# Two fused layers on one core: weights first, head stacks built in place, expert choice without the wide reciprocal, projections over four banks

## The chip, the cores and the metric

One core of one Trainium2 chip. The metric is the device time of one execution of the program, in microseconds; the median of several runs is compared.

## What is computed

The input x is 8 batches of 512 tokens with 128 features. Each batch goes through two pre-norm layers, `x = x + L(layernorm(x))`, in f32.

```
attention layer (A), 16 heads, DH = 8:
  Q = split(x); K = split(x @ Wk + bk); V = split(x @ Wv + bv)
  o = softmax(Q K^T + causal) V
  y = x + gelu(o) @ Wf + bf
mixture layer (F), 8 heads of 64, 8 experts:
  q, k = x @ w_q, x @ w_k
  gates = sigmoid(x @ w_gate); sel = argmax over the experts, per head and token
  values = chosen gate * (x @ value_expert[sel])
  out = softmax(q * 0.125 k^T, causal) values
  y = sum over heads of chosen gate * (out @ output_expert[sel])
```

## The kernel before

The program is written out by hand, engine by engine, with counting semaphores: each engine runs its own list, and a semaphore counts on over all batches. Nothing reorders the work; the tables at the top (`BANK`, `VALUES_AT`, `MAX_AT`, `HOTS_AT`, `OUTPUTS`) say after which unit another layer's or batch's piece is put in. A batch runs: attention A, `turn` (gelu and projection back), `experts` with `project_f` on TensorE (the mixture layer's gates, q and k, and the expert values), attention F, in which the next batch's layer A is prepared; the output experts' products of the mixture layer are spread over attention F and the next batch's attention A. The last batch's products stand at the end.

Precision is made from parts. Scores of A: q and k are split into three bf16 parts, written to DRAM (`parts_to_dram`) and read back as stacks of 72 rows (`restack_q`, `restack_k`), with three rows more for the negated maxima and their ones (`maxima_rows`, L350). Scores of F: q and k are each split into a high half, made by ScalarE (L926), and a low half, made by VectorE (L1276), in `pt`; `restack_f` (L339) sends both from there to four stacks: `s1q` (q high, q low), `s1k` (k high twice), `s2q` (q high) and `s2k` (k low), heads in pairs, 12 DMAs a pair, always to rows 0 to 63 and 64 to 127. `score` multiplies `s1` over 128 rows and `s2` over 96 rows, of which 64 and 65 hold the maxima and the ones and the rest zeros. The A stacks lie in the same memory as `s1q` and `s2k`. The scores are computed twice, once to find maxima and sums (`max_unit`, then `denominators` on ScalarE, L819), once for the exp (`score_unit`, L877).

`project_f` walks eight projections, u = 0 to 7, query and key by turns; each needs a PSUM bank (`BANK`), and `free` makes TensorE wait until the bank's last content was drained. Projections have banks 0 and 1; the 32 expert value units have banks 0 to 3. Of each value unit VectorE copies the tokens that chose the expert (`copy_predicated`, L1303), for which it needs `hot`, the one-hot choice. `gate_ops` makes this in VectorE's list, two steps after each of the first four low halves: add 1, reciprocal of 256 columns, largest gate, equals it, times a rank, largest rank, one-hot, cast. The one-hot goes by a transpose to DRAM and is repeated over 64 partitions (`repeat_hots`, L798) for `choose` (L1153) which multiplies the attention's output with it.

GpSimd does the causal select of the exp (L999), the powers for the norms (L981), residuals (L989), and the gates' product with the values (`gated_values`, L1007).

At the start SyncE loads x and layer A's weights, then constants to DRAM; GpSimd sets `s2q` and `s2k` to zero, VectorE `s1q`. The mixture layer's weights are loaded by SyncE behind the first stacks (L412, the value experts are 2 MB into `oe_sb`) and split into halves at group 2 of the first batch's attention A:

```
                for g in range(GROUPS):
                    if g == SPLIT_AT and k == "A" and b == 0:
                        expert_weights_high()
```

ScalarE makes the high halves (L752 in the trace, since `copy` has one line), VectorE the low ones (`expert_weights_low`, L1329).

## Time and profile before

| | us |
|---|---|
| median of 3 runs | 1398.5 |
| lowest, highest | 1398.37, 1403.59 |
| the profiled execution | 1397.98 |
| its span, first to last instruction | 1395.9 |
| TensorE / VectorE / ScalarE / GpSimd busy | 1165.2 / 903.2 / 894.2 / 211.3 |
| one steady batch | about 164 |

The page gives busy time by engine, the span in 40 slices, the DMA queues, the chain that ended last and the costliest groups of instructions. A steady batch shows in the trace as about 65 us of attention A with the turn, 54 of experts and 44 of attention F. All times are of one execution; "idle before" is time in which an engine had nothing it could start, and the name behind the arrow is what ended it.

### The profile page before, as it was taken

The numbers are of one execution on the slowest core, as the hardware profiler recorded it, in microseconds if no ns is written. First come the engines' busy times: TensorE is split into PE (matmuls) and PEld (weight loads), VectorE is DVE, ScalarE is ACT, GpSimd is POOL, SyncE is SP. The second block draws the span as 40 slices with busy tenths as digits, with TensorE's granted clock in tenths as the row PEclk, the third lists the DMA queues.
The fourth block names the chain that finished last, engine by engine and source line by source line (L and its number), as shares of the span: only waits on it lengthen the run. The fifth ranks groups of instructions, "written<-read, shape, count | busy, mean of one in ns | idle before, by whom it ended". The sixth has DMA issues, their size and how long they took to land.

```text
span 1395.9 us, 19696 instructions
## 1 busy us (share of the span) xinstructions
PE 1165.2 (83%) x5720; PEld 644.5 (46%) x5720; DVE 903.2 (65%) x2786; ACT 894.2 (64%) x2551; POOL 211.3 (15%) x264
## 2 busy tenths in 40 slices
PE   2556988888988899888897898888898888978988
PEld 1114753356533564246642475335643356424753
DVE  5552857748575775747677585765858577674855
ACT  1694376935779266962769548793678827696370
POOL 3011011201112012020111102120111211111010
PEclk9987999999999999999999999999999999999999
DMA  2401733126421553206432073413642155320723
GB/s 78 132 2 63 179 93 91 37 68 149 113 56 34 123 130 99 60 6 153 118 82 62 25 177 89 95 32 82 148 105 52 34 140 128 84 62 11 175 67 71
DMA packets 64177, 122.32 MB, mean 88 GB/s; under 512 B 14099, under 2 KB 29843, under 8 KB 59683
## 3 DMA queue, kind: packets, MB, share of 16 engines
q1 hardware_dynamic: 58950, 87.50, 25.0%
q10 hardware_dynamic: 5120, 33.56, 10.8%
q8 instruction: 46, 0.75, 0.2%
q14 instruction: 61, 0.50, 0.1%
HBM read 61.11 MB, written 9.06 MB: 50 GB/s over the span
## 4 chain that ended last, share of the span: by engine, by line
PE 41%; DVE 20%; ACT 19%; issue 14%; POOL 3%; DMA 2%; SPq 1%; ACTq 0%; DVEq 0%; POOLq 0%
ACT masked L819 9%; ACT pt L877 8%; PE ps_m L605 7%; PE ps_o L596 7%; DVE masked L1103 6%; PE ps_m L431 3%; PE ps_exp L512 3%; PE ps_m L433 2%; PE ps_max L700 2%; PE ps_m L432 2%; PE ps_exp L513 2%; PE ps_exp L431 2%; POOL pt L999 2%; DVE val L1303 2%; DVE at L1153 2%
## 5 line engine op out<-in xcount | busy, mean ns | idle before, releaser
L1103 DVE CUSTOM_DVE_ANT_0 masked<-ps_max,mask 128x512 f32<-128x512 f32 (+3 forms) x768 | 353.1, 486 | 206.7 <-PE ps_max L511 92.1
L819 ACT ACTIVATE masked<-masked,low 128x512 f32<-128x512 f32 (+3 forms) x768 | 426.2, 558 | 72.2 <-DVE low L1103 68.1
L877 ACT ACTIVATE pt<-ps_exp 128x384 f32<-128x384 f32 (+1 forms) x480 | 248.0, 523 | 103.7 <-PE ps_exp L513 66.6
L999 POOL TENSOR_SCALAR_AFFINE_SELECT pt<-pt 128x512 f32<-128x512 f32 (+2 forms) x192 | 134.6, 701 | 709.2 <-ACT pt L877 709.2
L605 PE MATMUL ps_m<-at,oe_sb 128*128 128x512 f32 x416 | 219.9, 618 | 5.7 <-DVE at L1153 3.5
L596 PE MATMUL ps_o<-pt,val 128*32 128x128 f32 (+6 forms) x1536 | 185.5, 459 | 19.7 <-POOL pt L999 19.1
L511 PE MATMUL ps_exp<-s1q,s2k 96*128 96x384 bf16 (+3 forms) x384 | 103.6, 319 | 67.8 <-ACT pt L877 54.5
L511 PE MATMUL ps_max<-s2k,s1q 96*128 96x512 bf16 (+3 forms) x512 | 138.8, 320 | 21.0 <-DVE low L1103 11.9
L1153 DVE TENSOR_TENSOR at<-osb,hots 128x512 f32<-128x512 f32 x208 | 145.3, 704 | 15.7 <-PE ps_m L605 15.7
L819 ACT ACTIVATION_READ_ACCUMULATOR masked<-masked,low 128x1 f32 x768 | 149.4, 195 | 0.0
L511 PEld LDWEIGHTS ps_exp<-s1q,s2k 96*128 96x128 bf16 x384 | 32.6, 99 | 185.1 <-ACT pt L877 140.1
L512 PE MATMUL ps_exp<-s1q,s1k 128*128 128x256 f32 (+2 forms) x256 | 100.7, 404 | 14.4 <-issue 12.4
L1303 DVE COPY_PREDICATED val<-osb,ps_exp 128x512 f32<-128x512 uint32 x128 | 92.0, 734 | 26.8 <-PE ps_exp L433 26.8
L596 PEld LDWEIGHTS ps_o<-pt,val 128*32 128x32 f32 (+1 forms) x1536 | 52.5, 119 | 103.3 <-issue 51.6
L511 PEld LDWEIGHTS ps_max<-s2k,s1q 96*128 96x128 bf16 x512 | 48.9, 100 | 97.0 <-DVE low L1103 47.7
L605 PEld LDWEIGHTS ps_m<-at,oe_sb 128*128 128x128 f32 x416 | 70.6, 193 | 39.4 <-DVE at L1153 27.6
L512 PE MATMUL ps_max<-s1k,s1q 128*128 128x256 f32 (+2 forms) x256 | 86.1, 346 | 1.3 <-DVE low L1103 1.3
L926 ACT ACTIVATE pt<-ps_m 128x512 fp32r<-128x512 f32 x64 | 38.3, 598 | 72.8 <-PE ps_m L433 71.2
L513 PE MATMUL ps_max<-s2k,s2q 96*128 96x256 f32 (+2 forms) x256 | 84.2, 339 | 0.0
L513 PE MATMUL ps_exp<-s2q,s2k 96*128 96x256 f32 (+2 forms) x256 | 83.7, 337 | 0.0
L512 PEld LDWEIGHTS ps_exp<-s1q,s1k 128*128 128x128 f32 x256 | 50.2, 196 | 67.5 <-issue 46.9
L1324 DVE TENSOR_TENSOR x<-ps_max,x 128x512 f32<-128x512 f32 x8 | 5.5, 692 | 101.7 <-PE ps_max L700 101.7
(159 smaller groups left out, 1837.9 us busy)
## 6 DMA issues: line engine op xcount, KB each, us to landing
hots<-hot_d ACTq DMA_DIRECT2D x64, 512.0 KB, 6.6
s1q<-pt SPq DMA_DIRECT2D x128, 128.0 KB, 2.3
s1k<-pt SPq DMA_DIRECT2D x128, 128.0 KB, 2.3
s1q<-parts_q SPq DMA_DIRECT2D x96, 96.0 KB
s2k<-parts_k SPq DMA_DIRECT2D x96, 96.0 KB
s2q<-pt SPq DMA_DIRECT2D x64, 128.0 KB, 2.3
s2k<-pt SPq DMA_DIRECT2D x64, 128.0 KB, 2.3
parts_q<-pt SPq DMA_DIRECT2D x24, 128.0 KB, 2.3
```

The source lines that it names most:

```text
L431: mm(dst, lh, rh, start=True, stop=False)
L511: return mm(dst, l1[0:KROWS, h, l2], r1[0:KROWS, h, r2], start=True, stop=True)
L512: mm(dst, l1[0][:, h, l2], r1[0][:, h, r2], start=True, stop=False)
L513: return mm(dst, l1[1][0:KROWS, h, l2], r1[1][0:KROWS, h, r2], start=False, stop=True)
L596: last = mm(ps_o[g % 2][j * w:j * w + w, qt * P:S], val[:, kt, h * w:h * w + w], pt[:, (n % 2) * 4 + j, c0:c1], start=kt == 0, stop=kt == 3)
L605: mm(ps_m[1][:], oe_sb[:, u], chosen_o(u), start=u == 0, stop=u == T * E - 1).then_inc(at_used.sem, 1)
L819: last = nc.scalar.activation(e, e, ACT.Exp, bias=low[:, g % 2, c:c + 1], scale=-1.0, accum_out=den[:, g % 2, c:c + 1])
L877: nc.scalar.activation(pt[:, (n % 2) * 4 + j, 0:c1 - c0], score_bank(k, u)[:, c0:c1], ACT.Exp).then_inc(exp_done[k].sem, 1)
L999: nc.gpsimd.affine_select(out=v, in_=v, compare_op=ALU.is_ge, fill=0.0, base=0, pattern=[[0, HG[k]], [0, m], [1, P]], channel_multiplier=- ...
L1103: last = v.tensor_tensor_reduce(out=masked[:, u % JUNK, c0:c0 + w], in0=src[:, c0:c0 + w], in1=mask[:, S - w:S], scale=-1.0, scalar=POS, o ...
L1153: v.tensor_tensor(chosen_o(u), osb[:, u // E], hots[:, u // E % 2, u % E], ALU.mult).then_inc(at_done.sem, 1)
L1303: v.copy_predicated(val[:, t].rearrange("p (h k) -> p h k", k=64), pick, ps_m[BANK[("F", "moe1", n)]][:].rearrange("p (h k) -> p h k", k=6 ...
```

## The change

- **Beginning.** The mixture layer's weights are loaded right after layer A's, ahead of the constants, and split before the first attention. The zeroing of `s1q`, `s2q` and `s2k` goes; a DMA fills rows 0 to 63 of `s2q` with zeros once, and SyncE sends k's parts only when it has landed. The ones of A's key stack are loaded again with each group; the zeros of its query stack are not loaded.
- **Fewer rows.** `score` multiplies only the rows in use: 72 or 75 in A, 64 and 66 or 128 in F.
- **In-place stacks.** Odd heads lie with their halves swapped, so that half of each stack is on the partitions on which it is made. GpSimd copies q high and k high (`copy_rows`), ScalarE q high into `s2q`, VectorE writes k low straight into `s2k`, in two instructions of 64 partitions. SyncE sends four DMAs a pair, not twelve.
- **Choice.** The expert of the least 1 + exp(-z) is taken; the reciprocal is of 32 columns, behind the one-hot. The gate steps stand one projection sooner; the largest logit is read later, and the last batch's output sum later.
- **Banks.** Projection u goes to bank u % 4.
- **Bytes.** The one-hot rows are bytes, with room for all four groups; all repeats are issued in attention F, none in A.

```diff
+SENDS, COPIES = 4, 4
 WRITES = 2 * PARTS
 MROWS = {"A": PARTS, "F": 2}
+X_ROWS = 64, 0
+ROWS = slice(0, 64), slice(64, P)
...
+BANK.update({("F", "qk", u): u % 4 for u in range(8)})
...
-HOTS_AT = {("F", 1): 0, ("F", 9): 1, ("A", 0): 2, ("A", 4): 3}
+HOTS_AT = {("F", 2): 0, ("F", 5): 1, ("F", 8): 2, ("F", 11): 3}
...
+            for dst, src in ((raw["wq"], wq), (raw["wkf"], wkf), (raw["wg"], wg),
+                             (ve_raw, ve.rearrange("p (e n) -> p e n", n=S))):
+                sp.dma_start(dst, src).then_inc(w_in[2].sem, 16)
             sp.dma_start(zeros_d, consts[5:9]).then_inc(cst.sem, 16)
             sp.dma_start(ones_d, consts[0:2]).then_inc(cst.sem, 16)
             sp.dma_start(onesb_d, consts[2:5].bitcast(BF16)).then_inc(cst.sem, 16)
-            sp.wait_ge(cst.sem, cst.count(0, 16 * 3))
-            sp.wait_ge(set_p.sem, set_p.count(0, 3))
-            sp.dma_start(ks[STACK:STACK + PARTS], onesb_d.rearrange("p (h n) -> p h n", n=S)).then_inc(cst.sem, 16)
             sp.dma_start(bf_sb[:], bf.partition_broadcast(P)).then_inc(w_in[1].sem, 16)
             sp.dma_start(bv_sb[:], bv).then_inc(w_in[1].sem, 16)
             sp.dma_start(wf_sb[:], wf.rearrange("p (g d) -> p g d", d=D)).then_inc(w_in[1].sem, 16)
+            sp.wait_ge(cst.sem, cst.count(0, 16 * 3))
+            sp.dma_start(s2q[0:64].bitcast(F32).rearrange("p h n -> p (h n)"), zeros_d[0].partition_broadcast(64)
+                         ).then_inc(zero_rows.sem, 16)
...
-                    for ab in range(2):
-                        r, h = slice(64 * ab, 64 * ab + 64), 2 * p + ab
-                        for dst, src in ((s1q[0:64, h], qh), (s1q[64:128, h], ql), (s1k[0:64, h], kh),
-                                         (s1k[64:128, h], kh), (s2q[0:64, h], qh), (s2k[0:64, h], kl)):
-                            sp.dma_start(dst.bitcast(F32), src[r]).then_inc(pair_sent[p % 2].sem, 16)
+                    ql, kh = (pt[:, 4 * (p % 2) + n, :] for n in (1, 2))
+                    sp.wait_ge(qk_lo.sem, qk_lo.count(f, 2 * p + 1))
+                    for odd in range(2):
+                        sp.dma_start(s1q[ROWS[1 - odd], 2 * p + odd].bitcast(F32), ql[ROWS[odd]]
+                                     ).then_inc(pair_sent[p % 2].sem, 16)
+                    sp.wait_ge(qk_hi.sem, qk_hi.count(f, 2 * p + 2))
+                    for odd in range(2):
+                        sp.dma_start(s1k[ROWS[1 - odd], 2 * p + odd].bitcast(F32), kh[ROWS[odd]]
+                                     ).then_inc(pair_sent[p % 2].sem, 16)
 
             def maxima_rows(k, b, g):
...
-                            pe.wait_ge(pair_sent[g].sem, pair_sent[g].count(f, 16 * SENDS))
+                            stacks_made(f, g)
                         max_unit("F", f, g, m)
+
+            def stacks_made(f, p):
+
+                pe.wait_ge(pair_sent[p % 2].sem, pair_sent[p % 2].count(f, 16 * SENDS * (p // 2 + 1)))
+                pe.wait_ge(rows_copied.sem, rows_copied.count(f, COPIES * (p + 1)))
+                pe.wait_ge(s2q_made.sem, s2q_made.count(f, 2 * (p + 1)))
+                pe.wait_ge(qk_lo.sem, qk_lo.count(f, 2 * p + 2))
...
                 (l1, l2), (r1, r2) = rows, cols
                 if k == "A":
-                    return mm(dst, l1[0:KROWS, h, l2], r1[0:KROWS, h, r2], start=True, stop=True)
+                    n = STACK + PARTS if extra else STACK
+                    return mm(dst, l1[0:n, h, l2], r1[0:n, h, r2], start=True, stop=True)
+                n = (slice(0, 66), slice(0, P))[h % 2] if extra else ROWS[h % 2]
                 mm(dst, l1[0][:, h, l2], r1[0][:, h, r2], start=True, stop=False)
-                return mm(dst, l1[1][0:KROWS, h, l2], r1[1][0:KROWS, h, r2], start=False, stop=True)
+                return mm(dst, l1[1][n, h, l2], r1[1][n, h, r2], start=False, stop=True)
...
+                if f > 0:
+                    act.wait_ge(at_done.sem, at_done.count(f - 1, (p + 1) * E))
                 for a in range(2):
                     row = hot_d[(2 * p + a) * E:(2 * p + a + 1) * E].rearrange("e n -> (e n)")
-                    nc.scalar.dma_start(hots[64 * a:64 * a + 64, p % 2].rearrange("p e n -> p (e n)"),
-                                        row.partition_broadcast(64)).then_inc(hots_in[p % 2].sem, 16)
+                    nc.scalar.dma_start(hots[64 * a:64 * a + 64, p].rearrange("p e n -> p (e n)"),
...
+                        act.wait_ge(rows_copied.sem, rows_copied.count(f, COPIES * (u // 2 - 1)))
                     nc.scalar.activation(pt[:, 4 * (u // 2 % 2) + 2 * (u % 2)].bitcast(F32R),
                                          ps_m[BANK[("F", "qk", u)]][:], ACT.Copy,
                                          scale=(SCALE, 1.0)[u % 2]).then_inc(qk_hi.sem, 1)
+                    if u % 2 == 1:
+                        p = u // 2
+                        qh = pt[:, 4 * (p % 2)].bitcast(F32R)
+                        act.wait_ge(qk_hi.sem, qk_hi.count(f, u))
+                        for odd in range(2):
+                            copy(s2q[ROWS[odd], 2 * p + odd], qh[ROWS[odd]]).then_inc(s2q_made.sem, 1)
...
+            def copy_rows(f, p):
+
+                qh, kh = (pt[:, 4 * (p % 2) + n].bitcast(F32R) for n in (0, 2))
+                pool.wait_ge(qk_hi.sem, qk_hi.count(f, 2 * p + 1))
+                for n, (dst, src) in enumerate(((s1q, qh), (s1k, kh))):
+                    if n == 1:
+                        pool.wait_ge(qk_hi.sem, qk_hi.count(f, 2 * p + 2))
+                    for odd in range(2):
+                        nc.gpsimd.tensor_copy(dst[ROWS[odd], 2 * p + odd], src[ROWS[odd]]).then_inc(rows_copied.sem, 1)
+                        pool.wait_ge(rows_copied.sem, rows_copied.count(f, COPIES * p + 2 * n + odd + 1))
+
...
+                step(1, v.tensor_scalar(g_w, g_s, 1.0, None, ALU.add))
+                after(1)
+                step(2, v.tensor_reduce(wlow[:], by_head(g_w), AX.X, ALU.min))
+                yield
+                after(2)
+                step(3, v.tensor_tensor(by_head(g_s), by_head(g_w), wlow[:].unsqueeze(2).to_broadcast([P, T * 8, E]),
+                                        ALU.is_le))
+                after(3)
+                step(4, v.tensor_tensor(by_head(g_s), by_head(g_s), rank[:].unsqueeze(1).to_broadcast([P, T * 8, E]),
+                                        ALU.mult))
+                yield
+                after(4)
+                step(5, v.tensor_reduce(wmax[:], by_head(g_s), AX.X, ALU.max))
+                after(5)
+                step(6, v.tensor_tensor(by_head(hot), by_head(g_s), wmax[:].unsqueeze(2).to_broadcast([P, T * 8, E]),
+                                        ALU.is_equal))
+                yield
+                after(6)
+                v.tensor_copy(hot_b, hot.rearrange("p (t c) -> p t c", c=64)).then_inc(gt_ready.sem, 1)
+                step(7, v.reciprocal(gmax[:], wlow[:]))
+                yield
+
+            def log_gates(f):
+
                 dve.wait_ge(gate_ready.sem, gate_ready.count(f, 1))
                 v.tensor_reduce(zmax[:], by_head(ps_m[BANK[("F", "gate", 0)]][:, 0:256]), AX.X, ALU.max
                                 ).then_inc(gate_exp.sem, 1)
-                step(1, v.tensor_scalar(g_w, g_s, 1.0, None, ALU.add))
-                yield
-                after(1)
-                step(2, v.reciprocal(g_s, g_w))
-                yield
-                after(2)
-                step(3, v.tensor_reduce(gmax[:], by_head(g_s), AX.X, ALU.max))
-                yield
-                after(3)
-                step(4, v.tensor_tensor(by_head(g_w), by_head(g_s), gmax[:].unsqueeze(2).to_broadcast([P, T * 8, E]),
-                                        ALU.is_ge))
-                yield
-                after(4)
-                step(5, v.tensor_tensor(by_head(g_w), by_head(g_w), rank[:].unsqueeze(1).to_broadcast([P, T * 8, E]),
-                                        ALU.mult))
-                yield
-                after(5)
-                step(6, v.tensor_reduce(wmax[:], by_head(g_w), AX.X, ALU.max))
-                yield
-                after(6)
-                step(7, v.tensor_tensor(by_head(hot), by_head(g_w), wmax[:].unsqueeze(2).to_broadcast([P, T * 8, E]),
-                                        ALU.is_equal))
-                yield
-                after(7)
-                v.tensor_copy(hot_b, hot.rearrange("p (t c) -> p t c", c=64)).then_inc(gt_ready.sem, 1)
...
                 gates = gate_ops(f)
+                next(gates)
                 for u in range(8):
                     dve.wait_ge(qk_hi.sem, qk_hi.count(f, u + 1))
                     hi = pt[:, 4 * (u // 2 % 2) + 2 * (u % 2)]
                     lo = pt[:, 4 * (u // 2 % 2) + 2 * (u % 2) + 1]
-                    v.scalar_tensor_tensor(out=lo.bitcast(F32R), in0=ps_m[BANK[("F", "qk", u)]][:],
-                                           scalar=(SCALE, 1.0)[u % 2], in1=hi, op0=ALU.mult, op1=ALU.subtract
-                                           ).then_inc(qk_lo.sem, 1)
-                    if u == 0 and f > 0:
+                    src = ps_m[BANK[("F", "qk", u)]]
+                    if u % 2 == 0:
+                        v.scalar_tensor_tensor(out=lo.bitcast(F32R), in0=src[:], scalar=SCALE, in1=hi, op0=ALU.mult,
+                                               op1=ALU.subtract).then_inc(qk_lo.sem, 1)
+                    else:
+                        even, odd = ROWS
+                        v.tensor_tensor(s2k[even, u - 1], src[even], hi[even], ALU.subtract)
+                        v.tensor_tensor(s2k[odd, u], src[odd], hi[odd], ALU.subtract).then_inc(qk_lo.sem, 1)
+                    if u < 3:
+                        next(gates)
+                    if u == 2:
+                        log_gates(f)
+                    elif u == 3 and f > 0:
                         outputs_end(f - 1)
-                    if u < 4:
-                        next(gates)
-                        next(gates)
-                    if u == 0:
-                        log_gates(f)
```

In the order of VectorE's list, the start of a steady batch's experts (`ps_m0`, `ps_m1`, `ps_exp0`, `ps_exp1` are banks 0 to 3). Before, from the log gates to the first predicated copy:

```order
L1255 SCALAR_TENSOR_TENSOR zabs<-zlow,zmax 128x32
L1276 SCALAR_TENSOR_TENSOR pt<-ps_m1,pt 128x512
L1229 TENSOR_REDUCE gmax<-osb 128x32
L1232 TENSOR_TENSOR osb<-osb,gmax 128x256
L1276 SCALAR_TENSOR_TENSOR pt<-ps_m0,pt 128x512
L1236 TENSOR_TENSOR osb<-osb,rank 128x256
L1240 TENSOR_REDUCE wmax<-osb 128x32
L1276 SCALAR_TENSOR_TENSOR pt<-ps_m1,pt 128x512
L1243 TENSOR_TENSOR osb<-osb,wmax 128x256
L1247 CAST osb<-osb 128x256
L1303 COPY_PREDICATED val<-osb,ps_exp0 128x512
```

The last low half stands three rows ahead of the first predicated copy. Now, the same place:

```order
L1267 TENSOR_REDUCE wmax<-osb 128x32
L1269 TENSOR_TENSOR osb<-osb,wmax 128x256
L1309 SCALAR_TENSOR_TENSOR pt<-ps_exp0,pt 128x512
L1273 CAST osb<-osb 128x256
L1274 RECIPROCAL gmax<-wlow 128x32
L1280 TENSOR_REDUCE zmax<-ps_max0 128x32
L1283 TENSOR_SCALAR zlow<-zmax 128x32
L1285 SCALAR_TENSOR_TENSOR zabs<-zlow,zmax 128x32
L1313 TENSOR_TENSOR s2k<-ps_exp1,pt 64x512
L1314 TENSOR_TENSOR s2k<-ps_exp1,pt 64x512
L1200 TENSOR_TENSOR at<-ps_max1,x1_0 128x512
L1338 COPY_PREDICATED val<-osb,ps_exp0 128x512
```

The one-hot and its cast are done before the last low half, which is two instructions, and the output sum of the last batch has moved behind it. GpSimd's list between the two attentions of a batch was the two powers and the four products; now it is:

```order
L1005 TENSOR_TENSOR rstd<-veps,half 128x4
L1035 COPY s1q<-pt 64x512 x2
L1035 COPY s1k<-pt 64x512 x2
L1035 COPY s1q<-pt 64x512 x2
L1035 COPY s1k<-pt 64x512 x2
L1005 TENSOR_TENSOR rstd<-veps,half 128x4
L1035 COPY s1q<-pt 64x512 x2
L1035 COPY s1k<-pt 64x512 x2
L1035 COPY s1q<-pt 64x512 x2
L1035 COPY s1k<-pt 64x512 x2
L1043 TENSOR_TENSOR val<-val,gmax 128x512 x4
```

All sixteen copies stand ahead of the first product.

## Rows read from the trace of the kernel before

**Rows 1.** The page, part 1: busy time by engine, share of the span, instructions.
```profile
PE 1165.2 (83%) x5720; PEld 644.5 (46%) x5720; DVE 903.2 (65%) x2786; ACT 894.2 (64%) x2551; POOL 211.3 (15%) x264
```

**Rows 2.** The chain of waits in order of time, first batch: start, us, what.
```profile
53.38 10.32 issue
...
94.70 3.52 ACT ve_h L752
```

**Rows 3.** SyncE's queue, first batch: start, us to issue, line, transfer, count.
```profile
22.03 2.63 SPq L301 DMA_DIRECT2D parts_k<-pt  x3
...
43.32 0.72 SPq L412 DMA_DIRECT2D oe_sb<-in_ve  x1
...
51.08 20.85 SPq L350 DMA_DIRECT2D s1q<-mt_a  x6
```

**Rows 4.** The DMA issues: transfer, queue, count, KB each, median us to landing.
```profile
hots<-hot_d ACTq DMA_DIRECT2D x64, 512.0 KB, 6.6
...
oe_sb<-in_ve SPq DMA_DIRECT2D x1, 2048.0 KB, 19.1
oe_sb<-in_oe SPq DMA_DIRECT2D x1, 2048.0 KB, 8.7
```

**Rows 5.** ScalarE by time: start, us, line, operation, [idle before <- what ended it].
```profile
37.30 0.72 ACT L819 ACTIVATE masked<-masked,low 128x512 f32<-128x512 f32 x1 [13.91 <-DVE low L1103]
...
64.31 0.60 ACT L877 ACTIVATE pt<-ps_exp 128x512 f32<-128x512 f32 x1 [8.66 <-PE ps_exp L511]
...
116.28 1.28 ACT L904 ACT_TABLE_LOAD   x1
...
737.03 1.08 ACT L877 ACTIVATE pt<-ps_exp 128x512 f32<-128x512 f32 x2 [0.99 <-DVE at L1153]
...
779.02 1.28 ACT L904 ACT_TABLE_LOAD   x1
```

**Rows 6.** One stretch, the experts of batch 4: busy us by engine, clock, DMA.
```profile
785.00:839.00 54.00, 47.77 (x207) 34.33 (x206) 42.01 (x113) 19.26 (x51) 4.64 (x5) 0.97 0.54 128
```

**Rows 7.** VectorE by time, experts of batch 4.
```profile
797.71 1.75 DVE L1226 RECIPROCAL osb<-osb 128x256 f32<-128x256 f32 x1
...
806.02 1.43 DVE L1303 COPY_PREDICATED val<-osb,ps_exp 128x512 f32<-128x512 uint32 x2 [2.27 <-PE ps_exp L433]
...
814.86 1.28 DVE L1276 SCALAR_TENSOR_TENSOR pt<-ps_m,pt 128x512 fp32r<-128x512 f32 x2
...
820.79 1.43 DVE L1303 COPY_PREDICATED val<-osb,ps_exp 128x512 f32<-128x512 uint32 x2 [1.37 <-PE ps_exp L433]
```

**Rows 8.** TensorE by time, experts of batch 4.
```profile
800.38 0.50 PE L431 MATMUL ps_m<-xh,wkf_h 128*128 128x512 f32 x1 [2.83 <-DVE pt L1276]
...
804.17 0.63 PE L433 MATMUL ps_m<-ve_l,xh 128*128 128x512 f32 x1
...
826.72 0.39 PE L512 MATMUL ps_max<-s1k,s1q 128*128 128x512 f32 x1
...
826.95 0.40 PE L513 MATMUL ps_max<-s2k,s2q 96*128 96x512 f32 x1
```

**Rows 9.** VectorE by time: the normalisation in batches 0 and 4, the split.
```profile
8.04 7.53 DVE L1047 TENSOR_SCALAR xnA<-x_sb,mv,rstd 128x128 f32<-128x128 f32 x4 [1.20 <-POOL rstd L981]
...
98.24 4.43 DVE L1329 TENSOR_TENSOR ve_l<-oe_sb,ve_h 128x4096 fp32r<-128x4096 f32 x1 [2.67 <-ACT ve_h L752]
...
813.86 1.08 DVE L1047 TENSOR_SCALAR xnA<-x_sb,mv,rstd 128x128 f32<-128x128 f32 x4
```

**Rows 10.** Groups by line and shape, GpSimd: busy us, mean ns, idle before.
```profile
L999 POOL TENSOR_SCALAR_AFFINE_SELECT pt<-pt 128x512 f32<-128x512 f32 x96 | 67.4, 702 | 441.5 <-ACT pt L877 441.5
```

**Rows 11.** GpSimd and VectorE by time, end of the first layer's attention, batch 4.
```profile
772.37 1.16 POOL L999 TENSOR_SCALAR_AFFINE_SELECT pt<-pt 128x1024 f32<-128x1024 f32 x1 [1.55 <-ACT pt L877]
772.50 1.58 DVE L1153 TENSOR_TENSOR xnA<-osb,hots 128x512 f32<-128x512 f32 x1
```

116 lines of the change are left out of this document (55 added, 61 removed).

## The prediction

> **What bounds the kernel.** Read the busy shares first [rows 1]: TensorE 83%, VectorE and ScalarE 65% and 64%. No engine is full, so the price of an edit depends on its stage. The sequence repeats every 164 us for eight batches; only the first batch and the end differ. I read three places.
>
> The first batch. The chain of waits [rows 2] has a hole of 10.32 us from 53.38 to 63.7, and later, at 94.70, the split of the expert weights. The hole: SyncE issues the 2 MB load of the value experts at 43.32 [rows 3], and it lands 19.1 us later, where the equal load of the output experts takes 8.7 [rows 4]. The maxima rows go into the same queue at 51.08, behind that load, and the scores that need them start at 63.7, when it has landed; ScalarE's first exp comes after 8.66 us of idling [rows 5].
>
> The experts stage, 785 to 839 in the fifth period [rows 6]: VectorE works 42.01 of 54 us and TensorE 47.77. Here VectorE sets the pace; its larger gaps are 2.27 us before the first predicated copy and 1.37 before value unit 18 [rows 7], and TensorE's big one is 2.83 us before the second key projection, which has no bank [rows 8].
>
> The first layer's attention: from the first exp to the table load 41.99 us in a steady batch (737.03 to 779.02), 51.97 in the first (64.31 to 116.28) [rows 5].
>
> **The beginning.** (a) The value experts are loaded first instead of after the stacks. The maxima rows find an empty queue: three of them are issued in about 2 us and land about 2 us later, near 55, not 63.7. That gives back the idle of 8.66 us. I take **-8.7** (ends -10.3, the hole, and -6.5, if another wait of 2 us, the length of one landing, shows behind it).
>
> (b) The split moves ahead of the attention. In the first batch it held ScalarE for 3.52 us with one tensor [rows 2] and VectorE for 4.43 [rows 9], with the maxima's negation and so the next group queued behind. The first batch's attention was 51.97 - 41.99 = 9.98 us longer than a steady one, although it has no products in it: **-10.0** (ends -11 and -8, the 3.52 and 4.43 alone). In its new place the split needs about 4.9 us of ScalarE and 6 of VectorE. ScalarE is idle for 13.91 us before 37.30 [rows 5], and VectorE's first maximum comes just before that; if the load came later than about 25 us, this cover would be gone and each us late would show.
>
> (c) The front itself. Without the two memsets the normalisation needs 1.08 us instead of 7.53 [rows 9], so the compute chain is some 7.7 us earlier. But SyncE then waits for three small constants that stand behind 2.5 MB of weights, and next fills 64 partitions of s2q with 1 MB of zeros, on which the key parts wait. The load issued near 4.7 lands near 15.4 if it takes 8.7; the zeros are like two of the 512 KB repeats, 6.6 us [rows 4], so near 22.5; the key parts went at 22.03 before [rows 3]. Nothing is won, about a us is lost: **+1.5**. Ends: -6 (constants and zeros slip between the weights) and +9 (the load takes its old 19.1 us).
>
> **Each batch, experts stage.** The walk starts from the gates' end, which stays (ScalarE's exp ends at 794.84). VectorE: the 256 wide reciprocal, 1.75, becomes a 32 wide one, which I put at 0.2 (at one column a cycle, 1.75 x 32/256 = 0.22), so -1.55. Four of the eight low halves become two instructions on 64 partitions. The time goes with the 512 columns, so each adds about 0.62 (two in a row took 1.28, [rows 7]): +2.5. Net +0.95 us.
>
> Against this, four banks let TensorE do all of the first four projections from 794.25 to 797.5. VectorE then runs without a gap: two gate steps, low, two steps, low low, two steps, low, cast, reciprocal, the three log steps, low low at about 801.6 to 802.9, the last batch's output sum to 803.6, and the first predicated copy follows at 803.6 instead of 806.02. From there it is bound by VectorE: ten copies at 0.70 and 1.25 of statistics end at 811.8 instead of 813.9, **2.1 earlier**. The fifth projection's low half waits for them and the normalisation, as before; the doubled low half of the sixth holds TensorE's next bank 0.6 longer, and 1.6 are left at value unit 18 (819.15, was 820.79, [rows 7]). The last doubled low half costs 0.65 in a stretch in which VectorE has no gap left. Left: **-0.95**. TensorE's slow stretch at 803 (0.63 us for a matmul that takes 0.39 at full clock, [rows 8]) I leave as it is; without it another 1.5 us would go.
>
> GpSimd now copies 16 pieces of 64x512 a batch, each near the 0.70 us of a 128x512 select [rows 10], and they run from 795.9 to 802 and 811.2 to 814: beside the gate steps and the normalisation. The trace shows such a meeting: an expert choice, both inputs in SBUF, took 1.58 us beside a select of 1.16 [rows 11], more than twice the 0.6 to 0.7 of an instruction of its size. So three gate steps of two SBUF inputs and four normalisations are exposed. From nothing to one whole copy each, 7 x 0.70 = 4.9; I take **+1.0**, a fifth, since GpSimd waits for a semaphore between copies. The Trainium skill, "SBUF — State Buffer", section "Who interferes with whom", has the rule: a VectorE instruction with two SBUF inputs, or in a two-port mode, blocks wholly against a GpSimd instruction that reads SBUF, and whoever issues first holds the ports. By that rule alone each of the seven could wait for one copy, 4.9 us a batch; it is the rival below.
>
> **Each batch, the rest.** ScalarE's eight copies into s2q are 8 x 0.60 = 4.8 us, under its idle in this stage (19.26 of 54 busy, [rows 6]); cover gone, the last two would delay the first denominators by 1.2. SyncE sends 16 rows of pairs, not 48. That was off the path; its store now waits for the later output sum, and the sends start at 804 instead of 800, with the fifth projection at 809.6 as their deadline. The DMAs of the maxima rows stay two a group. Two of the four groups of choice rows were repeated in 512 KB pieces in the first layer; now all four go in the second, as bytes. Such an issue at the start of the first layer held ScalarE's first exp for 0.99 us (737.03, [rows 5]); this goes in seven batches, and up to half may come back where four issues now stand in the second layer. **-0.5** (ends -1.0 and +0.6). A choice with bytes instead of bf16 I leave at its 0.69: nothing. The same for 72, 75, 64 or 66 rows instead of 96: a matmul of 128 rows takes 0.39, one of 96 rows 0.40 [rows 8].
>
> **The sum.** -8.7 - 10.0 + 1.5 = -17.2 once; -0.95 + 1.0 - 0.5 = -0.45 a batch, x 8 = -3.6. Against the profiled execution, 1397.98 us (span 1395.9), 1377.2; it lies 0.5 under the median of 1398.5, so I say **1378**. A measurement of this kernel can tell about 0.5%, 7 us.
>
> **Rivals.**
> *GpSimd in VectorE's way* (slower side). All seven exposed instructions wait a whole copy: -0.95 + 4.9 - 0.5 = +3.5 a batch, +28 in all, 1398 + 28 - 17 = 1409. It decides from 2.15 us a batch on. For it: the normalisation beside the memsets took seven times as long [rows 9]. Against: these were copies of 3.5 us, and some waits fall into VectorE's own gaps. 6%; half of it would give about 1393.
> *The load blocks the front.* Behind 2.5 MB the constants, the zeros and the parts come late, as the maxima rows did [rows 2]: (c) is +9, not +1.5, so 1386. For it: the 19.1 us. Against: those came with stacks of 24 partitions in the same queue; the load of the output experts alone took 8.7. 12%.
> *The experts stage gives more.* The fast start keeps TensorE at full clock (1.5 a batch) and the GpSimd copies cost little (1.0): -2.5 x 8 = -20 more at most, half of it likely: 1366. 20%.
> *The four banks do nothing*, because the fourth projection's low half comes at 803 either way: the 2.1 a batch are lost, +17, 1395. For it: the chain of low halves was VectorE's before. Against: 2.83 us of its gap were TensorE's. 7%.
>
> **How the numbers follow.** 55% for the forecast, 1371 to 1386, by (a) to (c) and +-0.7 a batch. The range takes in the third and most of the second and fourth: **1363 to 1392**. Under 1391.5 are the forecast, the larger gain, the late load, and little of the rest: faster 84%; the dead banks and half of the contention are within 0.5%: 11%; slower 5%.
>
> **What would show it.** First exp near 56 us, not 64.31, with no ve_h in the attention, and 42 us from it to the table load. First score near 37: at 30 (c) was too dark, at 45 the load blocked. In a steady batch: a predicated copy 2.4 us sooner behind the gates' exp (11.2 us before), last copy about 1 us sooner. Gate steps or normalisations over 0.6 us show the ports. A period of 163.5 instead of 164; above 166 the forecast is dead.

## The result, and the profile after

| us | before | after |
|---|---|---|
| median | 1398.43 (4 runs, 1395.87 to 1403.59) | **1437.4** (4 runs, 1432.73 to 1445.06) |
| span of the profiled execution | 1395.9 | 1438.0 |
| from one gates' exp to the next, typical | 164.1 | 170.3 |

The changed kernel takes 1.0277 times as long (95% interval 1.0241 to 1.0314), 39 us more, where the forecast was 20 less, with 1363 to 1392 as its range. Here and below the executions in the chip's slow state are left out of medians and ratios (1873 us in e_grouped, 2652 in e_no_pool, 1425 in e_two_banks, one of 1835 of the kernel before). The busy line, against [rows 1]:

```profile
PE 1242.4 (86%) x5720; PEld 648.3 (45%) x5720; DVE 926.9 (64%) x2817; ACT 932.7 (65%) x2615; POOL 284.9 (20%) x390
```

TensorE runs as many matmuls as before and is busy for 77 us more; VectorE has 24 us more. The groups by line and shape (busy us, mean ns of one, idle before) say which matmuls:

```profile
L532 PE MATMUL ps_max<-s2k,s2q 64*128 64x256 f32 x128 | 48.7, 381 | 0.0
...
L531 PE MATMUL ps_max<-s1k,s1q 128*128 128x256 f32 x128 | 43.1, 337 | 0.0
```

L532 in the max pass of the mixture layer has 64 rows now, and 256 columns take 0.381 us. The same two groups before:

```profile
L512 PE MATMUL ps_max<-s1k,s1q 128*128 128x256 f32 x128 | 35.4, 297 | 1.3 <-DVE low L1103 1.3
L513 PE MATMUL ps_max<-s2k,s2q 96*128 96x256 f32 x128 | 34.7, 291 | 0.0
```

The matmul that has 64 rows now had 96. The 128-row matmul beside it rose too, 0.297 to 0.337 us; about half of its group stands behind a 64-row one. TensorE and its weight loads by time, in the experts stage of batch 4, show how (start, us):

```profile
833.25 0.28 PE L531 MATMUL ps_max<-s1k,s1q 128*128 128x256 f32 x1
833.45 0.18 PEld L532 LDWEIGHTS ps_max<-s2k,s2q 64*128 64x128 f32 x1 [0.24 <-issue]
833.45 0.38 PE L532 MATMUL ps_max<-s2k,s2q 64*128 64x256 f32 x1
833.76 0.19 PEld L531 LDWEIGHTS ps_max<-s1k,s1q 128*128 128x128 f32 x1
833.76 0.38 PE L531 MATMUL ps_max<-s1k,s1q 128*128 128x256 f32 x1
834.08 0.18 PEld L532 LDWEIGHTS ps_max<-s2k,s2q 64*128 64x128 f32 x1
834.08 0.38 PE L532 MATMUL ps_max<-s2k,s2q 64*128 64x256 f32 x1
834.39 0.19 PEld L441 LDWEIGHTS ps_exp<-xh,wq_h 128*128 128x128 f32 x1
```

The kernel before, in the same stage:

```profile
827.89 0.28 PE L512 MATMUL ps_max<-s1k,s1q 128*128 128x256 f32 x1
827.89 0.19 PEld L513 LDWEIGHTS ps_max<-s2k,s2q 96*128 96x128 f32 x1
828.01 0.28 PE L513 MATMUL ps_max<-s2k,s2q 96*128 96x256 f32 x1
828.13 0.29 PE L512 MATMUL ps_max<-s1k,s1q 128*128 128x256 f32 x1
```

Each weight load now starts together with its own matmul; before, it started with the matmul ahead (827.89, its own at 828.01). So neighbours of 256 columns are 0.31 us apart, which were 0.12 apart. The 128-row matmul behind a 64-row one comes as late as the 64-row one.

The beginning, ScalarE by time, against [rows 5]:

```profile
55.52 1.06 ACT L895 ACTIVATE pt<-ps_exp 128x512 f32<-128x512 f32 x2
...
101.80 1.28 ACT L922 ACT_TABLE_LOAD   x1
```

The first exp comes at 55.52 (64.31 before), the reload of the table at 101.80 (116.28): 14.5 us won. VectorE in the experts stage, against [rows 7] and [rows 9]; the gates' exp starts at 802.28 here, at 794.45 before:

```profile
804.73 0.72 DVE L1263 TENSOR_TENSOR osb<-osb,rank 128x256 f32<-128x256 f32 x1
...
808.30 0.66 DVE L1273 CAST osb<-osb 128x256 bf16<-128x256 uint32 x1
...
811.88 0.72 DVE L1338 COPY_PREDICATED val<-osb,ps_exp 128x512 f32<-128x512 uint32 x1
...
820.75 1.80 DVE L1083 TENSOR_SCALAR xnA<-x_sb,mv,rstd 128x128 f32<-128x128 f32 x4
822.46 0.68 DVE L1309 SCALAR_TENSOR_TENSOR pt<-ps_m,pt 128x512 fp32r<-128x512 f32 x1
823.06 0.67 DVE L1313 TENSOR_TENSOR s2k<-ps_m,pt 64x512 fp32r<-64x512 f32 x1
823.75 0.69 DVE L1314 TENSOR_TENSOR s2k<-ps_m,pt 64x512 fp32r<-64x512 f32 x1
```

The first predicated copy is 9.60 us behind the gates' exp, was 11.57. One gate step took 0.72 and the cast 0.66, which were 0.41 and 0.29 before (the other gate steps kept their 0.41 and 0.42); the normalisation took 1.80, was 1.08 [rows 9].

### The profile page after: what moved, and what is told of

It reads as the page before. It is cut to its first block, busy times and chain, and to the rows that moved or that the text cites. A ratio compares the mean times of both kernels' runs of the same rounds, so it can differ in the third digit from the quotient of the medians.

```text
span 1438.0 us, 19787 instructions
## 1 busy us (share of the span) xinstructions
PE 1242.4 (86%) x5720; PEld 648.3 (45%) x5720; DVE 926.9 (64%) x2817; ACT 932.7 (65%) x2615; POOL 284.9 (20%) x390
## 4 chain that ended last, share of the span: by engine, by line
PE 44%; ACT 22%; DVE 15%; issue 10%; DMA 4%; POOL 2%; SPq 1%; ACTq 0%; DVEq 0%; POOLq 0%
ACT masked L838 12%; ACT pt L895 8%; PE ps_m L624 7%; PE ps_o L615 6%; PE ps_max L532 5%; PE ps_exp L441 3%; PE ps_max L531 3%; DVE masked L1139 3%; PE ps_m L441 3%; PE ps_exp L531 3%; DMA s2q<-mt_f 2%; PE ps_exp L443 2%; PE ps_exp L442 2%; PE ps_max L719 2%; PE ps_m L442 2%
## 5 line engine op out<-in xcount | busy, mean ns | idle before, releaser
L529 PE MATMUL ps_max<-s2k,s1q 72*128 72x512 bf16 (+3 forms) x512 | 139.9, 322 | 30.0 <-DMA s2k<-onesb_d 17.4
L529 PE MATMUL ps_exp<-s1q,s2k 75*128 75x384 bf16 (+3 forms) x384 | 105.4, 325 | 44.9 <-ACT pt L895 42.6
L532 PE MATMUL ps_max<-s2k,s2q 64*128 64x256 f32 (+2 forms) x256 | 108.3, 423 | 0.0
L529 PEld LDWEIGHTS ps_exp<-s1q,s2k 75*128 75x128 bf16 x384 | 32.8, 100 | 166.0 <-ACT pt L895 130.4
L529 PEld LDWEIGHTS ps_max<-s2k,s1q 72*128 72x128 bf16 x512 | 49.1, 101 | 103.9 <-issue 52.4
L531 PE MATMUL ps_max<-s1k,s1q 128*128 128x256 f32 (+2 forms) x256 | 89.9, 351 | 0.0
L441 PE MATMUL ps_exp<-ve_h,xh 128*128 128x512 f32 x128 | 62.0, 484 | 26.2 <-DVE s2k L1314 15.1
L532 PE MATMUL ps_exp<-s2q,s2k 66*128 66x256 f32 (+5 forms) x256 | 80.2, 324 | 0.0
L441 PE MATMUL ps_m<-ve_h,xh 128*128 128x512 f32 x128 | 60.4, 472 | 22.4 <-DVE pt L1309 15.6
```

The costliest lines, as they stand in the source:

```text
L441: mm(dst, lh, rh, start=True, stop=False)
L529: return mm(dst, l1[0:n, h, l2], r1[0:n, h, r2], start=True, stop=True)
L531: mm(dst, l1[0][:, h, l2], r1[0][:, h, r2], start=True, stop=False)
L532: return mm(dst, l1[1][n, h, l2], r1[1][n, h, r2], start=False, stop=True)
```

## The experiments

"Before" ran on the same chip beside each; its median was between 1395.8 and 1401.7. Times are medians, and each ratio is to that "before". The runs were made on several chips, so a difference between two of them holds that of the chips too. Where a size is given as a span, one end is from the medians and the other from the ratios.

### The 64 rows, and the beginning

**e_full_rows.** The changed kernel with more rows in the max pass; two transfers a batch zero the maxima rows first.

```diff
-                n = (slice(0, 66), slice(0, P))[h % 2] if extra else ROWS[h % 2]
+                n = (slice(0, 66), slice(0, P))[h % 2]
```

> The changed kernel, with the layer-F max pass at the full rows of the score pass (66 for even heads, 128 for odd ones) instead of 64; the maxima rows are zeroed for every batch by two more transfers, so the result stays the reference's. Theory 1 (TensorE pays at each 64-row matmul of the max pass and at the 128-row one behind it, 0.08 to 0.1 us each, 512 of them a batch over the 16 units of ... in all some 6 us a batch): the F max pass falls from 0.38 to 0.29 us a matmul of 256 columns, the time between the gates' exps from 170.3 to about 163.5, the median from 1437 to 1380 to 1385. Rival 2 (the loss sits in GpSimd's copies beside VectorE, or in the one transfer that now carries both maxima rows): the period stays near 170 and the median above 1430. Rival 3 (part of each): between 1390 and 1425.

(The 512 matmuls are those of the whole run: 256 of 64 rows and the ones behind them.) Measured: **1416.89**, ratio 1.0137 (1.0100 to 1.0174). The 256-column matmul fell to 0.283 us and TensorE's busy time to 1193.2, but the kernel won 20 us of the 52 to 57 that theory 1 had. The steady batches kept a period of about 170.8 us: of the 15.3 us between the profiled spans the seven periods hold 5.0 and the last batch 8.7. A new wait took a good part of the rest, of which e_full_hots tells below. Besides, the granted clock was lower in each of its executions, 0.926 to 0.936 against 0.946 to 0.970 in the changed kernel; what that cost was not tested.

**b_rows64.** The kernel before, with fewer rows in the same matmuls.

```diff
-                    last = score(k, dst[:], h, (Q[k], tile(3)), (KK[k], slice(0, S)))
+                    last = score(k, dst[:], h, (Q[k], tile(3)), (KK[k], slice(0, S)), N_MAX)
```

> The kernel before, with nothing changed but that the second matmul of each layer-F max tile takes rows 0 to 63 of its two stacks (rows 64 to 95 add nothing in that pass). Theory 1 (the 64 rows alone cost): its 256-column matmuls go from 0.29 to 0.38 us and the median from 1398 to 1435 to 1455, slower than the kernel before by about as much as the changed kernel loses. Rival 2 (the 64 rows only cost beside the new copies, or through the new waits): 1396 to 1402. A third outcome, under 1420 but above 1405, would say that they cost only where TensorE is what VectorE waits for.

Measured: **1498.93**, ratio 1.0712 (1.0656 to 1.0767). `N_MAX` is a name that the program sets again, to 12; the group shows it:

```profile
L514 PE MATMUL ps_max<-s2k,s2q 12*128 12x256 f32 x128 | 53.3, 416 | 0.0
```

So this is 12 rows (the low products of rows 12 and up are left out of the maxima), and it costs 102 us. The edit was made again with 64 and 65.

**b_rows64_true**, with a name of its own, 64.

> The kernel before with rows 0 to 63 in the second matmul of each layer-F max tile. In b_rows64 a name that the program sets again further down made them 12 rows (its rows show 12*128), at 0.416 us for 256 columns against 0.291 with 96 rows, and the run was 101 us slower. Theory 1 (fewer than some number between 64 and 66 rows costs, and fewer still costs more): 0.38 us for 256 columns and 1430 to 1460. Rival (only very few rows cost in this kernel, and the 64 rows cost in the changed kernel for another reason, such as the odd heads' rows 64 to 127): 1396 to 1405.

Measured: **1452.29**, ratio 1.0420 (1.0375 to 1.0465).

```profile
L514 PE MATMUL ps_max<-s2k,s2q 64*128 64x256 f32 x128 | 48.7, 381 | 0.0
```

The row is the changed kernel's to the last digit. With nothing else of the change, 64 rows instead of 96 cost 56 us.

**b_rows65**, the same with 65.

> The kernel before with 65 rows in the second matmul of each layer-F max tile (row 64 is zero on one side). 64 rows took 0.381 us for 256 columns and 4.2%, 66 and 96 take 0.283 to 0.291 us. If the step is between 64 and 65: 1394 to 1400 and 0.28 to 0.29 us. If it falls slowly with the rows: 0.37 us and over 1440.

Measured: **1403.18**, ratio 1.0041 (1.0020 to 1.0062).

```profile
L514 PE MATMUL ps_max<-s2k,s2q 65*128 65x256 f32 x128 | 34.9, 292 | 0.0
```

The step lies between 64 and 65 rows. The 0.4% that is left isn't explained.

**e_grouped.** The changed kernel; in two of the four tiles of a head the 64-row matmul goes first.

```diff
+                if narrow_first:
+                    mm(dst, l1[1][n, h, l2], r1[1][n, h, r2], start=True, stop=False)
+                    return mm(dst, l1[0][:, h, l2], r1[0][:, h, r2], start=False, stop=True)
```

> The changed kernel, with the same 64-row matmuls, but in two of four tiles of a head issued ahead of their 128-row partner, so that the order is 128, 64, 64, 128, 128, 64, 64, 128 and the height of the rows changes 4 times a head instead of 8. Version a of theory 1 (what costs is the change of height, in either direction): half of the loss comes back, 1408 to 1422. Version b (each 64-row matmul or its weight load is slow by itself, wherever it stands): 1432 to 1442, no change. In between the row of the page on these matmuls says which of the two orders is paid for.

Measured: **1449.03**, ratio 1.0365 (1.0320 to 1.0410): slower still. As a test it was badly laid out: value matmuls of 128 rows stand between the tiles, so the number of changes of height stayed as it was. Why it was 12 us slower is open; in its profile two of the seven periods took 180 us at a granted clock of 0.92, the others 170 to 172 at 0.97 to 0.99. The question was put again:

**b_rows64_twice.**

```diff
+                if n2 < KROWS:
+                    mm(dst, l1[1][0:n2, h, l2], r1[1][0:n2, h, r2], start=False, stop=False)
                 return mm(dst, l1[1][0:n2, h, l2], r1[1][0:n2, h, r2], start=False, stop=True)
```

> b_rows64_true with each of the 64-row matmuls of the layer-F max pass issued twice in a row, into the same sum (the low parts count twice in the maxima, which only steady the exponentials). In b_rows64_true a 64-row matmul starts 0.31 us (256 columns) behind the 128-row one before it, and the next 128-row one 0.31 behind it, where 0.12 is the distance of two of 96 and 128 rows. If what costs is the change of height: the second 64-row matmul starts 0.12 (0.23 for 512 columns) behind the first, and the added ones cost TensorE their columns only, 256 x about 0.16 = 42 us of its time, less of the kernel's: 1460 to 1490. If each 64-row matmul waits for the array to be empty, whatever stood before it: 0.31 (0.43), 256 x 0.36 = 92 us of its time and 1500 or more.

Measured: **1479.65**, ratio 1.0548 (1.0416 to 1.0680). TensorE by time, first this kernel, then b_rows64_true:

```profile
867.96 0.38 PE L513 MATMUL ps_max<-s1k,s1q 128*128 128x256 f32 x1
868.27 0.38 PE L515 MATMUL ps_max<-s2k,s2q 64*128 64x256 f32 x1
868.49 0.28 PE L516 MATMUL ps_max<-s2k,s2q 64*128 64x256 f32 x1
868.70 0.50 PE L432 MATMUL ps_m<-ve_h,xh 128*128 128x512 f32 x1
```

```profile
867.31 0.38 PE L513 MATMUL ps_max<-s1k,s1q 128*128 128x256 f32 x1
867.63 0.38 PE L514 MATMUL ps_max<-s2k,s2q 64*128 64x256 f32 x1
867.93 0.50 PE L432 MATMUL ps_exp<-ve_h,xh 128*128 128x512 f32 x1
```

From the 128-row matmul to the next one are 0.74 us with two 64-row matmuls between and 0.62 with one: the second costs 0.12, its columns and no more (it starts 0.22 behind the first and not 0.12, but the one behind it comes sooner by as much; the sum tells). The price is on the change of height: 0.62 against 0.24 for a pair of 128 and 96 rows, 0.38 for going down and up again, 0.19 a change. With 256 such matmuls in a run that is an estimate of 97 us of TensorE's time, of which the kernel before felt 56.

**b_begin.** The kernel before with the new beginning alone (weights first, split ahead of attention; memsets and constants as before).

```diff
             k_part1(0)
+            expert_weights_high()
             act.wait_ge(split_lo.sem, split_lo.count(0, 2))
```

> The kernel before with the new beginning alone: the four expert weights are sent for first and split ahead of attention. Forecast 10.0 for the split and 8.7 for the maxima rows, less 1.5 in front: 1381. If TensorE's granted clock falls behind its idle time in the beginning as in the changed kernel (0.50 from 25 to 100 us there, where before it was 1.00 to 80 us and the matmuls went to full speed at 75 us), first exp to the reload of the table takes 46 and not 42 us, and the median is 1383 to 1387. If the block of loads in front costs more than forecast: 1388 to 1395.

Measured: **1380.67**, ratio 0.9862 (0.9821 to 0.9903), 16 us less by the medians, 19 by the ratio. First exp 54.42, table reload 96.99:

```profile
96.99 1.28 ACT L902 ACT_TABLE_LOAD   x1
```

That is 42.6 us between the two, the 42 of the forecast and not the 46 that the expectation feared.

### Broadcasts, and the clock of the first 100 us

In e_full_rows the wait was for the maxima rows of the mixture layer. ScalarE, its DMA issues (ACTq), SyncE's (SPq) and TensorE by time:

```profile
863.26 0.45 ACTq L820 DMA_DIRECT2D hots<-hot_d  x1
...
863.67 0.25 ACT L774 ACTIVATE mt_f<-ps_m 16x128 f32<-16x128 f32 x1
863.75 0.85 ACTq L820 DMA_DIRECT2D hots<-hot_d  x1
...
863.95 1.44 SPq L363 DMA_DIRECT2D s2q<-mt_f  x2
...
871.33 0.80 PE L534 MATMUL ps_exp<-s1q,s1k 128*128 128x512 f32 x1 [3.86 <-DMA s2q<-mt_f]
```

The maxima rows, 4 KB a transfer, are issued until 865.39, right behind two broadcasts of 256 KB of the choice, and the scores wait for them until 871.33. The waits of TensorE, summed (us, times, longest):

```profile
PE ps_exp L534 <- DMA s2q<-mt_f: 28.1, 10, 4.2
```

**e_full_hots.**

```diff
-HOTS_AT = {("F", 2): 0, ("F", 5): 1, ("F", 8): 2, ("F", 11): 3}
+HOTS_AT = {("F", 0): 0, ("F", 3): 1, ("F", 6): 2, ("F", 9): 3}
```

> e_full_rows (the changed kernel with full rows in the layer-F max pass) with the four broadcasts of the choice issued by ScalarE in the layer-F stages 0, 3, 6 and 9 instead of 2, 5, 8 and 11. In e_full_rows the third and fourth stand 0.2 to 0.7 us ahead of the maxima rows: those were issued at 865.4 behind two broadcasts issued at 863.7 and 864.6, and the scores that need them started at 871.3, after 4.5 us of waiting; TensorE waits 28.1 us for them in all, 2.0 before. Theory 2 (broadcasts ahead of the maxima rows are the second cause): that wait falls under 6 us, the time between the gates' exps from 170.7 to 166 to 167.5, the median from 1417 to 1380 to 1393. Rival (the wait is for the rows' own transfer, now two rows in one): the wait stays near 28 us, the median over 1410.

Measured: **1399.29**, ratio 1.0030 (1.0007 to 1.0054), 15 to 18 less than e_full_rows; the wait fell to 9.8, not under 6. Theory 2 holds in its mechanism, though the median is 6 above its range: something of 19 to 23 us against b_begin is still there.

**e_hots_only**, the same edit on the changed kernel.

> The changed kernel with its 64-row matmuls, and the four broadcasts in stages 0, 3, 6 and 9 instead of 2, 5, 8 and 11. In the changed kernel TensorE waits only 5.9 us in all for the maxima rows, since the slow matmuls reach the rows' users late. Theory 2 gives back what the slow matmuls left of the wait: 1430 to 1437. If the two causes were independent: 1437 less 30 = 1407.

Measured: **1432.12**, ratio 1.0270 (1.0229 to 1.0310): 1 to 5 us, within noise, and far from the 30 of two independent causes. The slow matmuls hide the late rows.

**e_full_hots_warm.** 64 idle matmuls in TensorE's pause of the beginning.

```diff
+            for _ in range(64):
+                mm(ps_max[0][:], wv_h[:, 0:P], wv_h[:], start=True, stop=True)
```

> e_full_hots with 64 matmuls of 128x512 more, into a bank that nothing reads, in TensorE's idle stretch of the beginning (17.8 to 35.6). In every run with the weights in front the granted clock is 0.50 from 25 to 80 or 100 us, and the first attention's stretch from the first exp to the reload of the table takes 46.3 us, against 42.0 worked out for before, whose TensorE reached 0.22 us for 512 columns at 76 us. Theory 3 (the low clock is set by the idle stretch before it): with the filling the clock is 0.9 or more from 20 us on, attention's first matmuls are 0.23 and not 0.43 us apart, the first attention is 3 to 5 us shorter and the median 3 to 6 us below e_full_hots. Rival (the clock falls from power or from the new start, whatever TensorE did in between): clock still 0.50 to 0.67, medians equal within 3 us, or longer if the filling itself is in the way.

Measured: **1399.57**, ratio 1.0015 (0.9994 to 1.0035), the same as without. Stretches of its beginning (length, TensorE busy, weight loads, VectorE, ScalarE, GpSimd, granted clock, DMA share, GB/s):

```profile
20.00:30.00 10.00, 10.00 (x46) 8.27 (x45) 4.63 (x3) 0.00 (x0) 0.00 (x0) 1.00 0.44 116
...
40.00:60.00 20.00, 14.69 (x40) 3.54 (x39) 16.12 (x74) 19.79 (x71) 0.68 (x1) 0.50 0.20 66
60.00:80.00 20.00, 19.06 (x84) 5.82 (x84) 10.23 (x45) 19.25 (x64) 3.13 (x4) 0.50 0.01 2
```

The filling holds the clock at 1.00 while it lasts; in the attention behind it the clock is 0.50 as without it, and from first exp to table reload it takes 46.0 us in both. Theory 3 falls: the idle stretch isn't what slows the first attention. Nor does "every run with the weights in front" take 46.3: b_begin took 42.6 and e_full_rows 42.8.

### What is left: GpSimd, low halves, banks

All but the last are on e_full_hots, so against 1399.29.

**e_no_pool.** `copy_rows` goes; the sends become

```diff
-                        sp.dma_start(s1k[ROWS[1 - odd], 2 * p + odd].bitcast(F32), kh[ROWS[odd]]
-                                     ).then_inc(pair_sent[p % 2].sem, 16)
+                        for r in (1 - odd, odd):
+                            sp.dma_start(s1k[ROWS[r], 2 * p + odd].bitcast(F32), kh[ROWS[odd]]
+                                         ).then_inc(pair_sent[p % 2].sem, 16)
```

> e_full_hots (full rows, broadcasts moved; 1399 us, and still 18.6 above the kernel before with the new beginning) with GpSimd's copies done by transfers as before (8 sends a pair instead of 4). In the changed kernel VectorE's normalisation beside GpSimd takes 1.80 instead of 1.08, the multiply of a gate step 0.72 instead of 0.41, a cast 0.66 instead of 0.29, the reciprocal of 32 columns 0.33. Theory 4 (the shared port costs what the sum had: 1.0 a batch): VectorE's steps fall back, 8 x 1.0 to 1.7 off: 1386 to 1391. Rival (the copies' time is slack elsewhere, or the transfers cost what the port did): 1396 to 1402. If the sends in SyncE's queue were what counted, it would be slower than 1399.

Measured: **1377.99**, ratio 0.9859 (0.9831 to 0.9888): 21 to 24 us, 2.7 a batch or more. (There is no profile of it that can be read.)

**e_low_keys.**

```diff
-                        v.tensor_tensor(s2k[even, u - 1], src[even], hi[even], ALU.subtract)
-                        v.tensor_tensor(s2k[odd, u], src[odd], hi[odd], ALU.subtract).then_inc(qk_lo.sem, 1)
+                    v.scalar_tensor_tensor(out=lo.bitcast(F32R), in0=src[:], scalar=(SCALE, 1.0)[u % 2], in1=hi,
+                                           op0=ALU.mult, op1=ALU.subtract).then_inc(qk_lo.sem, 1)
```

> e_full_hots with the keys' low halves made in one VectorE operation of 128 rows and sent to the stack by transfers (6 sends a pair), as before, instead of two operations of 64 rows at 0.69 each. The sum had 2.5 a batch for the doubling, of which what lies behind the value copies counts. Theory 5 (it is paid in full where VectorE is the bound, 0.65 for each of the last two pairs, and TensorE also waits 1.9 for such a subtraction early): 1.3 to 2.5 a batch, 1380 to 1389. Rival (it is hidden by TensorE's value matmuls): 1395 to 1400.

Measured: **1373.71**, ratio 0.9824 (0.9796 to 0.9852): 26 to 29 us, 3.2 a batch or more, where VectorE's own time is 0.65 x 4.

**e_two_banks.**

```diff
-BANK.update({("F", "qk", u): u % 4 for u in range(8)})
+BANK.update({("F", "qk", u): u % 2 for u in range(8)})
```

> e_full_hots with the projections back on two banks. The first predicated copy stands 9.6 us after the gates' exp with four banks and 11.6 before; the sum had 0.65 a batch for it at the end of the stage. If that gain is real: 1402 to 1406, the first copy at 11 to 12 us. If it is used up by the later low halves: 1397 to 1401. If four banks harm (TensorE waits 1.88 and 2.12 for low halves in the value units, and its clock halves behind the second of these waits for 3.4 us): 1390 to 1396.

Measured: **1412.12**, ratio 1.0092 (1.0051 to 1.0132): four banks are worth 9 to 13 us, 1.1 to 1.6 a batch. The first predicated copy is back at 11.88 us behind the gates' exp.

**e_dma_stacks.** e_no_pool and e_low_keys, and ScalarE's copies of the queries' high halves sent by transfers too: 12 sends a pair.

> e_full_hots with every row of the stacks moved by transfers as before (12 sends a pair, no copies on GpSimd or ScalarE, the keys' low halves in one operation); what is left of the change is the beginning, the choice by least 1+exp(-z), the byte choice, four banks, and 72, 75, 66 or 128 rows. If theories 4 and 5 hold and add: 1399 less 8 x 2.3 to 4.2 = 1366 to 1381, at or below the kernel before with the new beginning (1381). If they share one limit, about 1385. If the loss left is in the broadcasts or the maxima rows: above 1392.

Measured: **1378.76**, ratio 0.9852 (0.9821 to 0.9883): in the range of theories 4 and 5, but no better than either edit alone.

**e_low_keys_no_pool.** The same, with ScalarE's copies kept: 10 sends a pair.

> e_low_keys (1374) and e_no_pool (1379) together: full rows, broadcasts moved, the keys' low halves in one operation and sent, and GpSimd's copies done by transfers (10 sends a pair); only ScalarE's copies of the queries' high halves stay. e_dma_stacks (1379), which does all of that and ScalarE's copies by transfers too, says that the two gains of 25 and 20 us don't add. If both take the same slack of the experts stage: 1370 to 1376. If the transfers give back what VectorE gains (SyncE's queue with 10 sends a pair): 1376 to 1382, and the wait for the maxima rows, 9.0 us in e_low_keys and 20.9 in e_dma_stacks, stands between them. If they add after all, and ScalarE's copies are what e_dma_stacks lost: 1355 to 1365.

Measured: **1359.89**, ratio 0.9736 (0.9708 to 0.9764), the fastest of all, 2.6% below the kernel before. The two edits add for the most part (39.4 of 46.9 us), and it is ScalarE's copies whose replacement by transfers costs 16 to 19. VectorE's normalisation, with nothing of GpSimd beside it, in groups by shape:

```profile
L1078 DVE TENSOR_SCALAR xnA<-x_sb,mv,rstd 128x128 f32<-128x128 f32 x32 | 8.8, 335 | 1.2 <-POOL rstd L1012 1.2
```

In the changed kernel that group stood at 13.8 us. The waits of this kernel, then those of e_dma_stacks:

```profile
PE ps_m L451 <- DVE pt L1303: 18.1, 8, 3.6
...
PE ps_exp L540 <- DMA s2q<-mt_f: 15.4, 11, 2.6
```

```profile
PE ps_m L452 <- DVE pt L1297: 27.4, 8, 4.9
PE ps_exp L540 <- DMA s2q<-mt_f: 20.9, 11, 4.8
```

By the code, ScalarE makes the fifth projection's high half only when the first pair's sends have landed, and its low half and TensorE come behind it. With two sends more a pair TensorE's wait there is 9.3 us longer in a run, and the one for the maxima rows 5.5. These two waits are the likely cause; no run takes them apart.

**e_narrow_low_keys**, the edit of e_low_keys on the changed kernel as it is.

> The changed kernel as it is, 64-row matmuls and broadcasts included, with the keys' low halves in one VectorE operation and sent by transfers. The same edit took 25.6 us off the kernel with full rows. If the two costs share the stage (TensorE is the bound while the rows are few): 1426 to 1435. If they add: 1408 to 1416.

Measured: **1425.14**, ratio 1.0217 (1.0170 to 1.0264): 8 to 12 us, less than half of what it gives with full rows. They share the stage for the most part.

## Why the prediction was wrong

**The step that failed** is the last sentence of "Each batch, the rest": "The same for 72, 75, 64 or 66 rows instead of 96", priced at nothing from a row of 128 and a row of 96 rows [rows 8]. It is right for 72, 75, 66 and 65. It fails at 64: the weight load no longer runs ahead, 0.38 us of TensorE for each 64-row matmul, 256 of them. Alone this is 56 us (b_rows64_true), and 56 on top of b_begin's 1380.7 is 1437, the result. That this meets it so closely is luck: with the rows put back the changed kernel gains 20 us, and 33 with the broadcasts moved as well (e_hots_only against e_full_hots). The rest is the other costs below, less what the change gained elsewhere. Both rows that the step went by were on the same side of the step; the bound was not taken from both sides. The Trainium skill has a rule that bears on it, "TensorEngine Tiling (Array Packing)", sections "Available Configurations" and "Key Properties": the array also works as tiles of 64 or 32 rows, and changing that mode drains TensorE. If a matmul of 64 rows runs in such a mode, going there and back costs two drains each time; the trace agrees, 0.19 us a change, none between two 64-row matmuls. That the mode is the cause is inferred, since no run shows the mode itself. But a drain at 64 rows should have stood among the rivals.

**The sum's other terms.** The period became 170.3, where "above 166 the forecast is dead" stood. The beginning was to give 17.2 and gave 16 to 19 by itself (b_begin): its first exp came 9.9 us earlier (the forecast had 8.7 less 1.5), and from there to the table reload it took 42.6 us, 9.4 less than before (the forecast had 10.0). In the changed kernel the first exp came at 55.52 for "near 56", the first score at 35.61 for "near 37", with no `ve_h` in the attention, but to the reload it took 46.3 us, not 42. The new beginning does not force this: e_full_rows has the same one and took 42.8. What differs is TensorE's clock in the last part. b_begin, then the changed kernel (the clock is the third number from the end):

```profile
80.00:100.00 20.00, 14.71 (x125) 5.20 (x125) 2.25 (x13) 18.50 (x45) 6.00 (x7) 0.91 0.31 110
```

```profile
80.00:100.00 20.00, 18.97 (x103) 5.64 (x101) 3.27 (x15) 15.36 (x42) 4.92 (x6) 0.59 0.29 107
```

It was 0.89 there in e_full_rows and 0.67 in e_full_hots, which took 46.0. Why it rose in one execution and not in another stays open.

The wide reciprocal: one of 32 columns was put at 0.2 us and took 0.34 (808.88). "One column a cycle" was no more than the scaling of 1.75 us by the columns, which the row does not bear out.

Low halves: +2.5 a batch in VectorE's time, of which the walk kept little behind the first copy; undoing it gives 3.2 or more with full rows, 1.0 to 1.5 in the changed kernel. GpSimd beside VectorE: +1.0, taken as a fifth; undoing it gives 2.7 alone, 1.7 beside e_low_keys. The rival's mechanism was there, at about half its price of 4.9; its place was right for the normalisation (1.80 instead of 1.08) and for one of the three gate steps (0.72 instead of 0.41), and the cast (0.66 instead of 0.29) it did not name. Four banks: "2.1 earlier" at the copies, of which the walk left 0.95 or so; the first copy came 2.0 sooner, and the banks are worth 1.1 to 1.6 a batch. The rival "four banks do nothing" is out.

The broadcasts: -0.5 a batch, with "up to half may come back". The sum asked what they hold on ScalarE, and not what is issued behind them on the other queue: with full rows their place costs 15 to 18 us, about 2 a batch. It hardly shows in the changed kernel, 1 to 5 us, behind the slow matmuls. The upper end, +0.6, was too low for the kernel with full rows.

So with the 64 rows away the forecast would still have failed: e_full_rows gives 1417, e_full_hots 1399. The low halves, GpSimd's copies and the broadcasts were all seen, but each was priced too low; in this stage 0.65 us of VectorE cost 0.8 of the stage. ScalarE's copies, taken as free, were rightly kept: against transfers they are worth 16 to 19 us. No run takes the gates' new steps or the byte choice on their own, so their shares are open. Together with the four banks, ScalarE's copies and the full rows' own transfers they make up the 18 to 21 us by which e_low_keys_no_pool lies below b_begin.

## What to carry to other kernels

Fewer rows in a matmul are not free of price because more rows have the same one: between 65 and 64 rows lies a step, and where matmuls of 64 and of 128 rows alternate, it is paid twice for each. Before a row count crosses it, keep a zero row in. A large broadcast that one engine issues just ahead of a small transfer that another waits for is read from the waits of that transfer's user, not from the issuing engine. And when one bottleneck is taken away, look at once at what had been hidden under it: here a second cost of 15 to 18 us showed only after the first was gone.
